# Last mixture's transfers spread over two queues, its tile table turned, and register loads without range asserts

## The reference, cut to what matters

```python
# first mixture (L1): two experts of 8 for each batch entry, F = 256
h = gelu(einsum('nd,edf->enf', xf, W1) + b1);  y = einsum('enf,efd->end', h, W2) + b2
# second mixture (L2): two experts of 8 for each token, F = 512, plus one shared expert
topw, topi = top_k(softmax(x @ Wr), 2)
# last mixture (L3): one expert of 32 for each token, F = 32
idx = argmax(xf @ router_w.T + router_b)
h   = relu(einsum('nd,ndh->nh', xf, W1[idx]) + b1[idx])
out = relu(einsum('nh,nhd->nd', h, W2[idx]) + b2[idx])
x   = x + out          # and that is the program's output
```

## Time and profile before

| | us |
|---|---|
| runs: median (lowest to highest) | 2392.99 (2389.83 to 2393.37) |
| the profiled execution's own time | 2382.97 |
| its span | 2381.2 |
| PE busy | 1778.7 (75%) |
| DVE busy | 1222.8 (51%) |
| ACT busy | 870.8 (37%) |
| POOL busy | 763.7 (32%) |
| mean granted TensorE clock | 0.83 |

### The profile page before, as it was taken

One profiled execution on the slowest core, in us unless ns is written; L12 is line 12 of the kernel. 1 busy time (PEld: TensorE's weight loads), 2 busy tenths in 40 slices (PEclk: granted clock), 3 DMA queues, 4 the chain that ended last, 5 costly groups with the idle time before them and its releaser, 6 DMA issues. The chain is left out here.

```text
span 2381.2 us, 46310 instructions
## 1 busy us (share of the span) xinstructions
PE 1778.7 (75%) x12847; PEld 1424.4 (60%) x12847; DVE 1222.8 (51%) x4445; ACT 870.8 (37%) x2627; POOL 763.7 (32%) x1119
## 2 busy tenths in 40 slices
PE   5658999967499667777776994599996777347873
PEld 4546777756489556666664773488886566224331
DVE  5663333389656566888886542222221788512110
ACT  2333444424366424444443431255543233112220
POOL 3430000034256451000001677244443255413332
PEclk8889999988799858999998997799999577555555
DMA  2100000011133200000002111366665421112222
GB/s 73 53 19 6 1 1 1 1 34 31 32 117 117 56 0 1 0 0 0 0 0 64 37 48 53 103 177 175 176 174 146 111 68 34 42 51 64 62 62 98
DMA packets 156917, 136.22 MB, mean 57 GB/s; under 512 B 27474, under 2 KB 130659, under 8 KB 156675
## 3 DMA queue, kind: packets, MB, share of 16 engines
q1 hardware_dynamic: 143170, 106.15, 15.9%
q0 software_dynamic: 13568, 27.98, 3.5%
HBM read 100.70 MB, written 37.54 MB: 58 GB/s over the span
## 5 line engine op out<-in xcount | busy, mean ns | idle before, releaser
L1429 ACT ACTIVATE FEAT<-BANKS,EXP 128x128 f32<-128x128 f32 x544 | 155.0, 368 | 230.4 <-PE BANKS L1406 229.5
L1047 ACT ACTIVATE EXP<-BANKS,NEGMAX 128x128 f32<-128x128 f32 x512 | 138.9, 382 | 191.3 <-DVE NEGMAX L1059 191.3
L1360 POOL DMA_INDIRECT scratch_made<-FEAT x136 | 130.2, 958 | 198.0 <-DVE FEAT L1489 194.8
L195 PE MATMUL BANKS<-ident,WA 128*128 128x128 f32 x256 | 61.5, 385 | 161.9 <-DVE WA L189 161.8
L1406 PE MATMUL BANKS<-FEAT 128*128 128x128 f32 x1088 | 153.0, 284 | 16.3 <-issue 8.0
L1489 DVE TENSOR_TENSOR FEAT<-BANKS,B2BC 128x128 f32<-128x128 f32 x136 | 39.6, 291 | 241.4 <-PE BANKS L1415 241.4
L1406 PEld LDWEIGHTS BANKS<-FEAT 128*128 128x128 f32 x1088 | 133.4, 193 | 34.8 <-issue 26.3
L1826 POOL DMA_INDIRECT scratch_made<-FEAT x96 | 91.9, 957 | 191.7 <-DVE FEAT L1985 169.5
L1415 PE MATMUL BANKS<-AUX,FEAT 128*128 x1088 | 152.5, 283 | 0.5 <-ACT FEAT L1429 0.4
L412 PE MATMUL BANKS<-FEAT,ident 128*128 128x256 f32 x588 | 149.9, 383 | 0.0
L195 PEld LDWEIGHTS BANKS<-ident,WA 128*128 128x128 f32 x256 | 42.0, 196 | 173.3 <-DVE WA L189 135.9
(11 more groups left out here) (353 smaller groups left out, 4572.5 us busy)
## 6 DMA issues: line engine op xcount, KB each, us to landing
FEAT<-in_L_ffn_W1p SPq DMA_DIRECT2D x136, 256.0 KB, 2.7
EXP<-in_L_ffn_W SPq DMA_DIRECT2D x128, 128.0 KB, 2.0
FEAT<-scratch_sent SPq DMA_DIRECT2D x136, 64.5 KB
STAGE<-in_adj SPq DMA_DIRECT2D x32, 256.0 KB, 2.8
EXP<-scratch_made SPq DMA_DIRECT2D x32, 256.0 KB, 3.6
FEAT<-scratch_sent SPq DMA_DIRECT2D x96, 65.5 KB, 1.8
scratch_sent<-NONE SPq DMA_DIRECT2D x64, 65.5 KB, 1.6
X<-in_x SPq DMA_DIRECT2D x16, 256.0 KB, 3.1
```

The costliest lines, as they stand in the source:

```text
L195: last = pe.transpose(tile(ps, k), tile(src, k), ident[:])
L1047: last = act.activation(tile(EXS[:, par], 4 * k + n), tile(PS[j], c), ACT.Exp, bias=NEGMAX[:, par, 4 * k + n:4 * k + n + 1])
L1360: pool.indirect_dma_start(out=made2, out_offset=bass.IndirectOffsetOnAxis(ap=XI_I[:, t % R_IN, H:ROW2], axis=0), in_=YO[:, t % R_OUT, :], ...
L1429: last = act.activation(tile(HR[:, t % R_H], c), tile(PS[2 + t % 2], c), ACT.Gelu, bias=BT[:, c, t:t + 1])
```

## The change

1. Every register load from a table (`value_load`) loses its `min_val` and `max_val`, on SP, PE and DVE, in ex1, ex2 and ex3.
2. In l3, `later` issues 4 of the 32 fills in each of its groups 1 to 8, instead of 32 in its group 0.
3. In ex3, the 32 blank tiles are written half by SP and half by ACT.
4. The table of tiles is made with tiles on partitions (128 x 32 elements a step). PE turns three columns of it into rows, and DVE copies them out of PSUM.
5. The down weights are issued by ACT, `second(t)` ahead of `norm(t)` in the same step. SP keeps `load` and `bias`.
6. The final copy goes in pieces of 8 KB for each of 128 rows, two transfers from SP and two from ACT.

```diff
-                        e = sp.value_load(EIDX[:, 2 * i + k:2 * i + k + 1], min_val=0, max_val=E1 - 1)
+                        e = sp.value_load(EIDX[:, 2 * i + k:2 * i + k + 1])
...
-                        for k in range(E3):
+                    if i >= 1 and i < 9:
+                        for k in range(4 * (i - 1), 4 * i):
                             sp.dma_start(sent3[...], NONE3[...]).then_inc(s.blank, 16)
...
-                for e in range(E3):
-                    r = sp.value_load(ZROW3[0:1, e:e + 1], min_val=0, max_val=ROWS3 - P)
+                for e in range(0, E3 // 2):
+                    r = sp.value_load(ZROW3[0:1, e:e + 1])
                     sp.dma_start(sent3[bass.ds(r, P), :], NONE3[:, e:e + ROW3]).then_inc(s.blank, 16)
-                sp.wait_ge(s.tab, 1)
+                sp.wait_ge(s.tab, 2)
...
-                in_turn(NT3, [(0, load), (2, second)])
+                in_turn(NT3, [(0, load), (2, bias)])     # bias(t): L1858's transfer at t % 4 == 3
...
+                pe.transpose(PS[5][0:E3, 0:NT3], OHT3[0:NT3, :], ident[0:NT3, 0:NT3])
+                pe.transpose(PS[5][0:1, 128:128 + NT3], EOF3[0:NT3, :], ident[0:NT3, 0:NT3])
+                pe.wait_ge(s.row, 1)
+                pe.transpose(PS[5][0:1, 256:256 + NT3], ROWF3[0:NT3, :], ident[0:NT3, 0:NT3]).then_inc(s.flip, 1)
...
+                def second(t):                            # on ACT
+                    q, j = t // 4, t % 4
+                    e = act.value_load(EOFI3[0:1, t:t + 1])
+                    if j == 0:
+                        reused(act, s.y_ps, q, 3)
+                    act.dma_start(W2D3[...], a["L3_ffn_W2"][bass.ds(e, 1)]...).then_inc(s_w3[q % 3], 16)
+                act.wait_ge(s.zr, 1)
+                for e in range(E3 // 2, E3):
+                    r = act.value_load(ZROW3[0:1, e:e + 1])
+                    act.dma_start(sent3[bass.ds(r, P), :], NONE3[:, e:e + ROW3]).then_inc(s.blank, 16)
+                act.wait_ge(s.tab, 2)
+                act.wait_ge(s.diag, 1)
                 act.wait_ge(s.bt, 1)
-                in_turn(NT3, [(0, norm), (3, hidden)])
+                in_turn(NT3, [(0, second), (0, norm), (3, hidden)])
...
-                v.tensor_tensor(GE3, TT3..., CUM3..., ALU.is_ge).then_inc(s.ge, 1)
+                v.tensor_scalar(LE3, CUM3[:], PIDX3[:, 0:1], None, ALU.is_le).then_inc(s.ge, 1)
+                v.scalar_tensor_tensor(PRP3, CUM3[:], PIDX3[:, 0:1], NTF3[:], ALU.is_le, ALU.mult).then_inc(s.prp, 1)
...
+                v.wait_ge(s.flip, 1)
+                v.tensor_copy(ROWI3[:], PS[5][0:1, 256:256 + NT3]).then_inc(s.tab, 1)
+                v.tensor_copy(EOFI3[:], PS[5][0:1, 128:128 + NT3]).then_inc(s.tab, 1)
+                v.tensor_copy(ONEH3, PS[5][0:E3, 0:NT3]).then_inc(s.oneh, 1)
...
+        out_v = out...rearrange("(g p n) -> g p n", g=4, p=P)     # made_v likewise
-                for g in range(4): sp.dma_start(flat[rows, :], made3[rows, :]).then_inc(s.stored, 16)
+                for g in range(2): sp.dma_start(out_v[g], made_v[g]).then_inc(s.stored, 16)
+            # on ACT: for g in range(2, 4): the same
```

More of the change, by code:

```diff
@@ L1772, in _ @@
                 in_turn(NG, [(1, norm), (3, shift), (0, combine), (0, stats), (6, place), (5, choice), (2, add), (4, top)])
-        s = sems("ex3", "tot ai bi nt b0 tri cu zr blank ge sel prp prv ex dd row oneh tab bb bt xn t_ps xT h_ps h hT_ps hT y_ps y "
+        s = sems("ex3", "tot ai bi nt b0 tri cu zr blank ge sel prp prv ex dd row oh flip oneh tab bb bt xn t_ps xT h_ps h hT_ps hT y_ps y "
                         "in0 in1 in2 in3 in4 in5 in6 in7 in8 in9 in10 in11 out0 out1 out2 out3 out4 out5 out6 out7 out8 out9 out10 out11 w2a w2b w2c diag b2sel b2out b2a b2b b2c")
@@ L1794, in program @@
         picked3 = nc.dram_tensor("scratch_picked3", (NT3, H), FP32, kind="Internal").ap()
[L1795 to L1801, removed]
+        ONEH3 = EXP[0:E3, 4900:4900 + NT3]
+        BT3 = EXP[:, 5000:5000 + NQ]
+        LE3, PRP3, OHT3 = (EXP[:, 4200 + 40 * k:4200 + 40 * k + E3] for k in range(3))
+        TOE3, PREV3, EOF3, DD3, ROWF3 = (EXP[:, 4400 + 4 * k:4400 + 4 * k + 1] for k in range(5))
         TRI3 = WA[:].rearrange("p a n -> p (a n)").rearrange("p (e f) -> p e f", e=E3)
@@ L1809, in program @@
         PIDX3 = lb("PIDX3", [P, 1])
[L1810 to L1811 removed]
+        EOFI3 = lb("EOFI3", [1, NT3], INT32)
+        ROWI3 = lb("ROWI3", [1, NT3], INT32)
         with nc.Block() as block:
@@ L1846, in _, with bias @@
                 sp.dma_start(picked3, B2SEL3).then_inc(s.b2out, 16)
-                sp.wait_ge(s.diag, 1)
                 sp.wait_ge(s.b2out, 16)
[L1850 to L1853, removed]
+                def bias(t):
+                    q = t // 4
+                    if t % 4 == 3:
                         reused(sp, s.y_ps, q, 3)
-                    sp.dma_start(W2D3[F3 * j:F3 * (j + 1), q % 3, j * H:(j + 1) * H], a["L3_ffn_W2"][bass.ds(e, 1)].rearrange("o f d -> (o f) d")
-                                 ).then_inc(s_w3[q % 3], 16)
-                    if j == 3:
                         sp.dma_start(B2S3[:, q % 3, :], picked3[4 * q:4 * q + 4, :].rearrange("(o k) d -> o (k d)", o=1)
                                      ).then_inc(s_b3[q % 3], 16)
-                in_turn(NT3, [(0, load), (2, second)])
+                in_turn(NT3, [(0, load), (2, bias)])
             @block.tensor
@@ L1868, in _ @@
                     pe.matmul(PS[6][F3 * j:F3 * (j + 1), 0:NQ], b1_3[:],
-                                     ONEH3[0:E3, :].rearrange("p (q j) -> p j q", j=4)[:, j, :], start=True, stop=True)
-                pe.matmul(PS[5][0:NT3, 0:H], ONEH3[0:E3, :], b2_3[:], start=True, stop=True).then_inc(s.bb, 1)
+                                     ONEH3.rearrange("p (q j) -> p j q", j=4)[:, j, :], start=True, stop=True)
+                pe.matmul(PS[4][0:NT3, 0:H], ONEH3, b2_3[:], start=True, stop=True).then_inc(s.bb, 1)
                 def turn(t):
@@ L1991, in program @@
         s = sems("out", "stored")
+        out_v = out.rearrange("b t h -> (b t h)").rearrange("(g p n) -> g p n", g=4, p=P)
+        made_v = made3[0:B * T, :].rearrange("r h -> (r h)").rearrange("(g p n) -> g p n", g=4, p=P)
         with nc.Block() as block:
@@ L1994, in _ @@
             def _(sp):
[L1995 to L1998, removed]
+                for g in range(2):
+                    sp.dma_start(out_v[g], made_v[g]).then_inc(s.stored, 16)
                 sp.wait_ge(s.stored, 4 * 16)
+            @block.scalar
+            def _(act):
+                for g in range(2, 4):
+                    act.dma_start(out_v[g], made_v[g]).then_inc(s.stored, 16)
         release()
```

37 lines of the change are left out of this document (16 added, 21 removed).

## The result

| | before | after |
|---|---|---|
| median of 5 runs, us (lowest to highest) | 2393.37 (2389.83 to 2397.13) | 2409.13 (2405.27 to 2410.71) |
| ratio after / before, 95% interval | | 1.0058 (1.0033 to 1.0082) |
| profiled execution: own time; span, us | 2382.97; 2381.2 | 2409.13; 2407.3 |

The kernel became 0.6% slower, where 2262 us was forecast. The last mixture did gain, as expected; the first two, which were to gain too, lost more than it gained. All of one profiled execution each.

A forecast was written before the change was run, and what follows sets the result against it. SP's instruction stream was taken as the bound. Savings of 44 + 13 + 6.5 + 22 + 45.5 = 131 us from the profiled 2383.0 gave 2252, or 2262 as median of runs (2393 - 131); range 2222 to 2303.

The forecast's parts named there:

- Asserts away, ex2: ex2: without range checks SP's transfer pair shortens, PE is late next, a tile takes 1.93 us, not 2.261; saves 44 us.
- nothing by themselves: PE's and DVE's streams: their checks stand beside matmuls already queued, so removing them was costed at nothing.
- Rival 3: SP's address of an unbounded register takes as much more arithmetic as the check took; 61 us lost, 2323 us; chance 0.06.
- Asserts away, ex1: ex1: without SP's range checks an entry falls from 2.28 to PE's 2.07 us; saves 13 us, bounds 6 to 18.
- Fills of l3: l3: spreading the 32 fills closes most of DVE's 7.08 us wait; saves 6.5 us, bounds 3 and 8.
- Head of ex3: Start of ex3: blanks halved between queues and unchecked start their last 22 us earlier; new table worth nothing by itself.
- Loop of ex3: ex3's loop: a quartet falls from 9.63 to 7.93 us and the first scatter comes sooner; together 45.5 us.
- The ring: ex3's loop: the 12-tile ring, loads waiting for scatters, is the longest next bound, 15.86 us per two quartets.
- so it hides: ex3's loop: ACT's `second` ahead of `norm` takes 0.85 us while tiles arrive 1.26 apart, so it costs nothing.
- Final copy: Copy at the end: transfers bound it, not the queue, so the change gives nothing; bounds -2 and +3 us.
- Rival 1: ex3's loop: PE's granted clock rises above 0.51, saving 17 us more, 2245 us; chance 0.18.

The follow-up runs named there:

- e3: The kernel before with the bounds taken off the four register loads of PE and DVE alone: ratio 1.0286.
- e1: The kernel after with bounds put back on the four register loads of PE and DVE, SP and ScalarE still bare: ratio 0.9514.
- e4: The kernel after with the range told to the compiler on PE and DVE but not tested at run time, so no check at all: ratio 0.9467.
- e2: The kernel before with the bounds taken off SP's seven register loads alone: ratio 0.9615.
- e5: e4 with ScalarE's `hidden` in ex3 one step later (lag 4 in place of 3): ratio 0.9407.
- e9: e5 with `second`, the issue of ex3's down weights, given back to SP: ratio 0.9509.
- e12: The kernel after itself, unchanged, run again beside the kernel before: ratio 1.005.
- e8: e4 with all 32 blank fills of ex3 issued by SP, the new table kept: ratio 0.9471.
- e6: e4 with the 32 blank fills of l3 issued together again, as in the kernel before: ratio 0.9479.

## Why the prediction was wrong

**Asserts away, ex2 (44).** The step that failed, in its own words: "The checks on PE's and DVE's own streams stand beside matmuls already queued: nothing by themselves." It has two faults. First, it took the checks to be gone. In e3 and in the kernel after, a load without bounds has its check at every use in an SBUF address instead, so in ex2 taking the bounds off moved it from one place into four. Rival 3 had an address that grows as much as the check took, but on SP, where it doesn't happen, and gave it 0.06. Second, "nothing by themselves" nearly holds for the one check at the load, 1.996 us a tile in e1 against 1.957 in e4, but not for one ahead of each pair of passes. The prediction gave PE 0.04 us a tile over its floor of 1.89, while a use now costs 0.178 + 0.018 of the sequencer ahead of two passes. That makes 2.60 a tile in place of 1.93. SP's half of the step was right: 43.9 us in e2, and PE's floor is 1.957 when all checks are gone (e4).

**Asserts away, ex1 (13).** Same fault, 26.4 the wrong way. Beyond it the bound was wrong: SP's 2.28 an entry looked like 2 x 1.10, but taking SP's checks away changed nothing (159.2; SP still starts an entry every 2.27 us in e2), while PE's own one a load, which was costed at nothing, held 11.1 us. SP's pitch equalled its cost because PE's pitch was nearly the same.

**Fills of l3 (6.5).** The named wait closed and the stretch didn't shorten beyond its spread. "DVE is the busiest engine there, so most of the hole closes" took the end of a wait for a gain; what was late next was not named, and the runs leave it open.

**Head of ex3 (22).** Right: 19.2. With the second queue 9.9, the checks 9.4, the table nothing. Of the 2.8 missing, SP's wait for the last blank to land explains part: 4.1 us, with both queues' fills landing up to 4.5 after issue where one alone had 1.6.

**Loop of ex3 (45.5).** Measured 27.1 (46.3 less 19.2). Two sentences failed: "The ring is longest" and, of `second` on ScalarE, "so it hides". What was costed was `second` ahead of a `norm` whose tile isn't there yet. Not seen was that `hidden`, which waits for PE's flip, stands ahead of both in ScalarE's order, and the next `down` behind them. In that circle `second` takes 0.58 us (2248.10 to 2248.68); no run puts it behind `norm` in the same step. Moving `hidden` by one step brings the ring, 15.40 for two groups where 15.86 was forecast. From e4 to e5 that is worth 10.2 us. PE's checks stand in the same circle and cost 12.8 in the kernel after: 10.2 for the one at the load (e1 to e4) and 2.6 more for its move to the use (after to e1). With both gone, ex3 has given 69.3 us (287.7 to 218.4) where 67.5 were forecast, but in a kernel that the forecast was not for.

**Final copy (0).** 1.3 us slower, inside its bounds. **Rival 1** didn't come: the loop's granted clock is 0.50 in the kernel after, at its lower level (1.2 GHz) as before. The sum had 2262 for this kernel; such a time belongs to another: e4, without any check, stands at 0.9467, 2266 us, with ex1 (-11.7), ex2 (-46.4) and the head (-19.3) near their forecasts.

The Trainium skill, DMA: Bandwidth & Descriptors, Latency and other measured facts, gives about 600 ns for a register load from memory. No trace here agrees: in the median it takes 0.27 us on SP, and on PE in ex2 0.30 in e1 and 0.35 in the kernel after. Going by the row was right.

## What to carry to other kernels

Before bounds are taken off a register load, see what the register addresses: here, for DRAM in a DMA on SP or ScalarE the check vanished, for SBUF in a matmul or a DVE operand it came back at every use. Tell the compiler the range and skip the test where the value is clamped anyway, and compare the count of asserts, not their source lines. Register work on PE hid beside queued matmuls when it came once a tile in ex2, and did not when it came ahead of every second pass; so count where it stands, not only how much it is. When an instruction is put into an in-order stream, look at every wait that stands ahead of it there, not only at its own length.

## What the runs showed that was not expected

The chip matters by more than this change. The kernel before ran at 2393 us in the first comparison and at 2396 on the chip of e9 to e12, but at 2463 and 2460 on those of e1 to e4 and e5 to e8. Most of the difference lies in one stretch that no edit touches, the layer ahead of ex2: 258 to 272 us in e1 to e8, 215.6 to 215.9 in every other profile. (The kernel before has a profile from the first comparison alone.) In the kernel before, then in e6 (columns as above):

```profile
1280.00:1495.70 215.70, 161.90 (x992) 121.70 (x992) 94.29 (x624) 64.49 (x113) 144.45 (x166) 0.86 0.19 57
```

```profile
1273.10:1544.80 271.70, 188.94 (x992) 139.48 (x992) 94.54 (x624) 63.53 (x113) 144.27 (x166) 0.78 0.15 45
```

The same instructions take 56 us more at a granted clock of 0.78 instead of 0.86. PE's busy time grows by only 27 of them, the rest is in none of the engines' busy times, and no run here tells what it is. This is why the experiments are set beside the kernel before on their own chip.
